# Two-layer graph network on one core: the second layer's scores, softmax and aggregation joined into one pass over batches of 11 blocks

## The chip, the core and the metric

The kernel runs on 1 core of one Trainium2 chip. The metric is the device time of one execution in microseconds. Engines are named as the profile names them: PE is the matrix engine, DVE the vector engine, ACT the scalar engine, POOL the general engine (here above all the issuer of gathers), SP the engine that issues the other transfers.

## The reference, cut to what matters

There are 3,125 nodes with 256 features and 50,000 edges sorted by destination. The first layer (gated messages, summed at the destination) isn't touched. The second layer is attention over the edges:

```python
Q, K, V = ((enh @ W + b).reshape(N, 4, 64) for W, b in ((Wq, bq), (Wk, bk), (Wv, bv)))
mod_k = K[src] + 0.2 * rel_w[edge_relations][:, None, :]
scores = jnp.einsum('ehd,ehd->eh', Q[dst], mod_k) / 64 ** 0.5
seg_max = jax.ops.segment_max(scores, dst, num_segments=N)
ex = jnp.exp(scores - seg_max[dst])
w = ex / jax.ops.segment_sum(ex, dst, num_segments=N)[dst]
agg = jax.ops.segment_sum(w[:, :, None] * V[src], dst, num_segments=N)
msgs = jnp.where(deg[:, None, None] > 0, agg, V)
out = msgs.reshape(N, 256) @ Wo + bo          # then + node_features, layer norm
```

## The kernel before

Edges come in chunks of 256, nodes in windows of 128. A block is one chunk seen against one window; there are 220 blocks, and all edge work runs block by block. Every engine has its own program, written out by hand: `pipeline(engine, stages, count, body)` runs steps u = 0, 1, 2, ..., and in step u each stage of the list, in the order of the list, works on block u minus its lag. So the order of the list is the order in which an engine meets its waits, and a wait at one stage holds all stages behind it, those of the next step too. `after(engine, signal, n)` waits until n signals have come.

The second layer has these parts:

- Projection (L1160 to L1171): K, V and Q of each window. `[K V]` rows go to a table in DRAM (L343), Q stays in SBUF in a high and a low part.
- Scores (220 blocks). SP loads one row of destinations and edge types (L353) and writes the gathered values back to DRAM as `block_values` (L358). POOL gathers 256 rows of `[K V]`, two gathers of 128 rows a block (L430), into 4 slots. PE spreads the row over the partitions (L1183 on), DVE compares it with the partition number to get one-hots (L903), PE adds keys and relations and picks the queries, ACT copies the keys out of PSUM (L643), DVE multiplies (L911) and sums each head's 64 products (L917).
- Softmax over all edges at once (L932 to L964): scores are turned into rows, running maxima go forth and back over each row, carries between rows are added, then one exponential.
- Aggregation (220 blocks). SP brings the values back (L372), DVE weights them (L974), ACT makes the one-hots of the destinations in two steps (`distances1`, L662, and `one_hot1`, L668) and copies the weights beside the values (L656), PE sums with the one-hot, DVE adds the sum to the window's row of `agg` (L982 reads the window's number into a register, L986 adds). The buffers are rings of 5 blocks.
- Output: POOL adds a bias to all of `xs` (L512), scales `agg` (L516), then windows go through the last projection and the norm.

On PE nearly all matmuls are recorded at one helper's line, L1042, transposes at L1045; an f32 product shows as two MATMUL records, an f32r product as one.

Of the kernel before, what the change touches and what calls it, by code (L numbers as in the profile page):

```python
# [13 lines left out]
P = 128  # L14
HEAD = HID // HEADS
CHUNK = 256
# [12 lines left out]
RING = 5  # L29
SHARES = 64  # L30
AGGW = HID + HEADS
assert CHUNKS % 2 == 0 and BLOCKS % SLOTS == 0 and BLOCKS % (2 * RING) == 0


def build(nc, x, src, dst, etype, ea, w1, wg, b_cat, w2, b2, ln0, query_col, wqkv, b_qkv, rel, wo, b_o, ln1, out):
# [6 lines left out]
    kv_tab = nc.dram_tensor("kv_tab", (WPAD * P, 2 * HID), f32, kind="Internal").ap()  # L42
    block_values = nc.dram_tensor("block_values", (BLOCKS // 2, P, 2, 2 * HID), f32, kind="Internal").ap()
    row_tab = nc.dram_tensor("row_tab", (BLOCKS, 2 * CHUNK), bf16, kind="Internal").ap()

    ctx = ExitStack()
    with ctx:
# [13 lines left out]
        ident_r = sb(ctx, "ident_r", [P, P], f32r)  # L61
# [11 lines left out]
        dst_row = sb(ctx, "dst_row", [HALF_B, 2, CHUNK], f32)  # L73
        chunk_i = sb(ctx, "chunk_i", [1, BLOCKS], i32)
        win_i = sb(ctx, "win_i", [1, BLOCKS], i32)
        ends_row = sb(ctx, "ends_row", [HEADS, 2, BLOCKS], f32)
        idx = sb(ctx, "idx", [P, 2, SLOTS, 2], i32)
# [5 lines left out]
        gath = sb(ctx, "gath", [P, SLOTS, 2, 2 * HID], f32)  # L83
# [3 lines left out]
        with l0:  # L87
            w_node = sb(l0, "w_node", [P, 2, 2 * HID], f32)
# [38 lines left out]
            row_b = sb(l0, "row_b", [HALF_B, 2, 2, CHUNK], bf16)  # L127
# [3 lines left out]
        with l1:  # L131
            agg = sb(l1, "agg", [P, WINDOWS, AGGW], f32)
            exp_col = sb(l1, "exp_col", [P, BLOCKS, 2, HEADS], f32)
            rel_parts = sb(l1, "rel_parts", [P, HID], f32r)
            spread = sb(l1, "spread", [P, P], bf16)
            block_row = sb(l1, "block_row", [P, SLOTS, 2, CHUNK], bf16)
            rel_sb = sb(l1, "rel_sb", [P, HEAD], f32)
            wo_hi = sb(l1, "wo_hi", [P, 2, HID], f32r)
            wo_lo = sb(l1, "wo_lo", [P, 2, HID], f32r)
            qt = ExitStack()  # L140
            with qt:
                q_hi = sb(qt, "q_hi", [P, WPAD, HID], f32r)
                q_lo = sb(qt, "q_lo", [P, WPAD, HID], f32r)
                a0 = ExitStack()
                with a0:
                    wqkv_hi = sb(a0, "wqkv_hi", [P, 2, 3 * HID], f32r)
                    wqkv_lo = sb(a0, "wqkv_lo", [P, 2, 3 * HID], f32r)
                    b_qkv_sb = sb(a0, "b_qkv_sb", [P, 3 * HID], f32)
                    qkv_row = sb(a0, "qkv_row", [P, 2, 3 * HID], f32)
                a1 = ExitStack()  # L150
                with a1:
                    hot_t = sb(a1, "hot_t", [P, 2, 2, CHUNK], f32r)
                    key_sb = sb(a1, "key_sb", [P, 2, 2, HID], f32)
                    prod = sb(a1, "prod", [P, 2, 2 * HID], f32)
            a2 = ExitStack()
            with a2:
                s_row = sb(a2, "s_row", [HALF_B, 2, HEADS, CHUNK], f32)
                m_row = sb(a2, "m_row", [HALF_B, 2, HEADS, CHUNK], f32)
                edge_max = sb(a2, "edge_max", [HEADS, 2, BLOCKS], f32)
                run_max = sb(a2, "run_max", [HEADS, 2, BLOCKS], f32)  # L160
                carry = sb(a2, "carry", [HEADS, 2, BLOCKS], f32)
                carry_col = sb(a2, "carry_col", [HALF_B, 2, 2, HEADS], f32)
            a3 = ExitStack()
            with a3:
                values = sb(a3, "values", [P, RING, 2, 2 * HID], f32)
                weighted = sb(a3, "weighted", [P, RING, 2, AGGW], f32)
                dist1 = sb(a3, "dist1", [P, RING, 2, P], f32)
                hot1 = sb(a3, "hot1", [P, RING, 2, P], f32)
                v_in = sb(a3, "v_in", [P, 2, HID], f32)
# [5 lines left out]
                ln1_sb = sb(a3, "ln1_sb", [P, 2, HID], f32)  # L175

# [3 lines left out]
        wo_sb = arriving[:, 6 * HID:8 * HID].rearrange("p (c n) -> p c n", c=2)  # L180


        used = [0]
# [1127 lines left out]
```

## Time and profile before

| | us |
|---|---|
| median of 3 runs | 2142.18 |
| lowest and highest | 2140.08 and 2154.2 |
| the profiled execution, its own time | 2156.49 |
| its span in the profile | 2154.6 |
| PE busy | 1732.6 (80%) |
| DVE busy | 1645.5 (76%) |
| ACT busy | 1135.0 (53%) |
| POOL busy | 1043.5 (48%) |

Busy shares are averages over parts with different limits, so they are to be read part by part. Row times are microseconds from the span's start. Two instructions that stand back to back overlap a little, so what one costs its engine is the distance between two starts, and what a waiting engine sees is the whole duration.

### The profile page before, as it was taken

The page shows a single profiled execution, that of the slowest core. Times are in us where ns is not written, and L with a number is a line of the kernel's source. Part 1 is how long each engine was busy: PE and PEld are TensorE (multiplying, and loading weights), DVE is VectorE, ACT ScalarE, POOL GpSimd, SP SyncE. Part 2 cuts the span into 40 slices and gives each one's busy share as a digit, 9 for nine tenths or more (in the row PEclk, how much of TensorE's full clock was granted, in tenths as well). Part 3 has the DMA queues.
Part 4 walks back from the last instruction along what each step waited for, and adds up shares of the span by engine and source line. Part 5 has one row for each costly group of instructions (what it writes and reads, how often), then busy time and mean ns, then how long its engine had stood idle before and what let it go on. Part 6 is the DMA issues. An engine that isn't in the chain of part 4 may idle for free. (4 is left out here: it accounts for less than half of the span.)

```text
span 2154.6 us, 46785 instructions
## 1 busy us (share of the span) xinstructions
PE 1732.6 (80%) x10754; PEld 1502.2 (70%) x10810; DVE 1645.5 (76%) x3024; ACT 1135.0 (53%) x2898; POOL 1043.5 (48%) x1123
## 2 busy tenths in 40 slices
PE   6799999999999999935877667766777761999984
PEld 3699999999999999934655556555556551655554
DVE  5489889888899888897656666666666567888988
ACT  1377778777888777744411111111111111999953
POOL 0155555555566555559265556666656543000023
PEclk9999999999999999977998988898898995999998
DMA  4456656665666566611487888888888861766643
GB/s 120 169 165 179 179 169 176 174 178 162 178 181 180 163 176 176 175 42 49 145 256 235 242 239 247 249 248 249 245 240 249 250 205 56 234 224 225 230 132 99
DMA packets 203908, 403.45 MB, mean 187 GB/s; under 512 B 29103, under 2 KB 126312, under 8 KB 203880
## 3 DMA queue, kind: packets, MB, share of 16 engines
q0 software_dynamic: 70400, 230.74, 38.0%
q1 hardware_dynamic: 133480, 172.38, 23.9%
q8 instruction: 12, 0.20, 0.0%
q14 instruction: 16, 0.13, 0.0%
HBM read 328.28 MB, written 74.73 MB: 187 GB/s over the span
## 5 line engine op out<-in xcount | busy, mean ns | idle before, releaser
L430 POOL DMA_INDIRECT gath<-edge_in_tab,idx x440 | 464.8, 1056 | 349.1 <-DVE gate_in L816 188.4
L430 POOL DMA_INDIRECT gath<-kv_tab,idx x440 | 417.2, 948 | 275.5 <-issue 108.4
L1042 PE MATMUL bank<-gath,ident 128*128 128x256 f32 x880 | 313.9, 451 | 208.8 <-issue 111.6
L643 ACT COPY key_sb<-bank 128x512 f32<-128x512 f32 x220 | 125.3, 587 | 587.8 <-PE bank L1042 326.9
L1042 PEld LDWEIGHTS bank<-gath,ident 128*128 128x128 f32 x880 | 161.9, 220 | 256.0 <-issue 138.9
L911 DVE TENSOR_TENSOR prod<-bank,key_sb 128x512 f32<-128x512 f32 x220 | 151.3, 688 | 239.7 <-ACT key_sb L643 168.2
L1042 PE MATMUL bank<-weighted,hot 128*128 128x260 f32 x880 | 238.7, 403 | 36.2 <-DVE weighted L974 34.5
L1042 PE MATMUL bank<-w_lo,relu_hi 128*128 128x256 f32 x880 | 250.2, 284 | 0.0
L1042 PE MATMUL bank<-w_hi,relu_lo 128*128 128x256 f32 x880 | 249.8, 284 | 0.0
L1042 PE MATMUL bank<-w_hi,relu_hi 128*128 128x256 f32 x880 | 249.4, 283 | 0.0
L1042 PEld LDWEIGHTS bank<-weighted,hot 128*128 128x128 f32 x880 | 152.6, 191 | 122.3 <-ACT hot L668 57.6
L1042 PE MATMUL bank<-rel_parts,hot_t 128*128 128x256 f32 x440 | 234.1, 532 | 0.0
L569 ACT ACTIVATE relu_hi<-bank 128x512 fp32r<-128x512 f32 x220 | 131.4, 597 | 170.4 <-PE bank L1042 155.2
L1045 PE MATMUL bank<-ident,gath 128*128 128x128 f32 x880 | 170.1, 275 | 23.4 <-DVE ea_parts L803 12.9
L830 DVE TENSOR_TENSOR msg_lo<-msg,msg_hi 128x512 fp32r<-128x512 f32 x220 | 152.9, 695 | 43.1 <-ACT msg_hi L581 21.3
L917 DVE TENSOR_REDUCE exp_col<-prod 128x512 f32 (+1 forms) x220 | 151.0, 686 | 31.2 <-issue 4.9
L974 DVE TENSOR_TENSOR weighted<-values,exp_col 128x512 f32<-128x512 f32 x220 | 163.0, 742 | 12.1 <-DMA values<-block_values 8.5
L1042 PEld LDWEIGHTS bank<-w_hi,relu_lo 128*128 128x128 f32 x880 | 169.8, 193 | 0.0
L825 DVE TENSOR_TENSOR msg<-bank,gate 128x512 f32<-128x512 f32 x220 | 151.2, 688 | 22.6 <-PE bank L1042 6.6
L1042 PEld LDWEIGHTS bank<-w_lo,relu_hi 128*128 128x128 f32 x880 | 168.4, 191 | 0.0
L1042 PEld LDWEIGHTS bank<-w_hi,relu_hi 128*128 128x128 f32 x880 | 168.4, 191 | 0.0
L903 DVE TENSOR_SCALAR hot_t<-bank,iota_part 128x512 fp32r<-128x512 f32 x220 | 163.2, 742 | 2.0 <-remote 2.0
(230 smaller groups left out, 4730.0 us busy)
## 6 DMA issues: line engine op xcount, KB each, us to landing
block_values<-gath SPq DMA_DIRECT2D x220, 256.0 KB
values<-block_values SPq DMA_DIRECT2D x110, 512.0 KB, 3.4
ea_in<-in_ea SPq DMA_DIRECT2D x440, 64.0 KB
gath<-edge_in_tab,idx POOLq DMA_INDIRECT x440
gath<-kv_tab,idx POOLq DMA_INDIRECT x440
edge_in_tab<-node_row SPq DMA_DIRECT2D x26, 256.0 KB, 2.0
kv_tab<-qkv_row SPq DMA_DIRECT2D x26, 256.0 KB, 2.0
block_row<-row_tab SPq DMA_DIRECT2D x220, 1.0 KB
```

The source lines that it names most:

```text
L430: g.indirect_dma_start(gath[:, q, i, :], None, table, bass.IndirectOffsetOnAxis(ap=idx[:, half, q, i:i + 1], axis=0)).then_inc(arrived[q], 16)
L569: s.activation(relu_hi[:, q % 2, :], bank[q % 2][:], ACT.Relu).then_inc(relu_hi_done, 1)
L643: s.copy(key_sb[:, q % 2, :, :].rearrange("p i f -> p (i f)"), bank[2 + q % 2][:]).then_inc(key_copied, 1)
L825: v.tensor_tensor(msg[:, q % 2, :], bank[4 + q % 2][:], gate[:, q % 2, :], ALU.mult).then_inc(msg_done, 1)
L830: v.tensor_tensor(msg_lo[:, q % 2, :, :].rearrange("p i f -> p (i f)"), msg[:, q % 2, :], msg_hi[:, q % 2, :, :].rearrange("p i f -> p (i ...
L903: v.tensor_scalar(hot_t[:, q % 2, :, :].rearrange("p k e -> p (k e)"), bank[q % 2][:], iota_part[:], None, ALU.is_equal).then_inc(hot_t_do ...
L911: v.tensor_tensor(prod[:, q % 2, :], bank[4 + q % 2][:], key_sb[:, q % 2, :, :].rearrange("p i f -> p (i f)"), ALU.mult).then_inc(prod_don ...
L917: v.tensor_reduce(out=exp_col[:, ds(b, 1), :, :].rearrange("p o i h -> p (o i h)"), in_=prod[:, q % 2, :].rearrange("p (j d) -> p j d", d= ...
L974: last = v.tensor_tensor(weighted[:, q % RING, :, 0:HID].rearrange("p i (h d) -> p i h d", h=HEADS), values[:, q // 2, q % 2, :].rearrange ...
L1042: return nc.tensor.matmul(out_, lhsT=lhs, rhs=rhs, start=start, stop=stop)
L1045: return nc.tensor.matmul(out_, lhsT=in_, rhs=ident[:], is_transpose=True, start=start, stop=stop)
```

## The change

Scores, softmax and aggregation become one pipeline over the 220 blocks. Gathered rows of `[K V]` (516 numbers instead of 512: each head's values are followed by a one, which sums the weights) stay in 22 slots in SBUF, until the block's values are weighted; 12 of the slots lie in `xs` and `hs`, which are stored in DRAM before and loaded again at the end. After each 11 blocks the scores, now 44 rows (block, head) of 256 edges, get local maxima, carries, and a running maximum that is passed on to the next batch; `agg` of the window that goes on is rescaled. Keys and queries are now held with features on the partitions: keys are transposed, and heads are summed by a product with `adder`. The row of destinations comes to all partitions by transfer. The core of the diff:

```diff
+BATCH = 11
+KEEP = 2 * BATCH
+BROWS = 2
@@ sync @@
+            sp.wait_ge(x1_done, WPAD)
+            sp.dma_start(rows_tab[0, :, :], xs[:].rearrange("p w f -> p (w f)")).then_inc(rows_saved[0], 16)
             pipeline(sp, [(store_keys_values, 0)], WPAD, 2)
+            sp.wait_ge(h2_done, WPAD)
+            sp.dma_start(rows_tab[1, :, :], hs[:].rearrange("p w f -> p (w f)")).then_inc(rows_saved[1], 16)
...
+                after(sp, hot_t_done, b - BROWS + 1)
+                for half in range(2):
+                    sp.dma_start(block_row[half * RELS:(half + 1) * RELS, slot, :, :].rearrange("p k e -> p (k e)"),
+                                 row_tab[ds(b, 1), half, :].to_broadcast([RELS, 2 * CHUNK])).then_inc(brow_in[slot], 16)
...
-            pipeline(sp, [(load_block_row, 0), (save_values, 3)], BLOCKS, SLOTS)
-            pipeline(sp, [(load_values, 0)], BLOCKS // 2, RING)
+            pipeline(sp, [(load_block_row, 0), (load_steps, 4)], BLOCKS, KEEP)
+            sp.wait_ge(query_fetched, BLOCKS)
+            sp.dma_start(hs_back[:].rearrange("p w f -> p (w f)"), rows_tab[1, :, 0:WINDOWS * HID]).then_inc(rows_back, 16)
+            sp.dma_start(xs_back[:].rearrange("p w f -> p (w f)"), rows_tab[0, :, 0:WINDOWS * HID]).then_inc(rows_back, 16)
+            sp.wait_ge(weighted_done, BLOCKS)
@@ gpsimd @@
+                after(pool, weighted_done, b - KEEP + 1)
+                after(pool, key_ready, b - BATCH + 1)
...
+            pool.wait_ge(rows_back, 2 * 16)
+            pool.wait_ge(ow_in, 4 * 16)
+            g.tensor_tensor(xs_back[:], xs_back[:], ln1_sb[:, 1:2, :].to_broadcast([P, WINDOWS, HID]), ALU.add).then_inc(beta1_added, 1)
@@ scalar @@
+            def fetch_query(k, q):
+                b = KEEP * k + q
+                w = act.value_load(win_i[0:1, ds(b, 1)], min_val=0, max_val=WINDOWS - 1)
+                after(act, query_ready, b - 1)
+                s.copy(q_now[:, q % 2, :, :].rearrange("p t f -> p (t f)"),
+                       q_tab[:, ds(w, 1), :, :].rearrange("p o t f -> p (o t f)")).then_inc(query_fetched, 1)
...
+            def distances1(k, q):
+                b = KEEP * k + q
+                after(act, agg_ready, b - 1)
+                for i in range(2):
+                    last = s.activation(hot1[:, q % 2, i, :], iota_node[:], ACT.Square, bias=rel_col[:, ds(b, 1), i], scale=-1.0)
+                last.then_inc(dist1_done, 1)
...
+            pipeline(act, [(fetch_query, 0), (copy_keys, 1), (copy_scores, 3), (copy_weights, 7), (distances1, 17), (one_hot1, 18),
+                           (exponents, 6)], BLOCKS, KEEP)
@@ vector @@
+                v.tensor_scalar(hot_t(q).rearrange("p k e -> p (k e)"), block_row[:, slot, :, :].rearrange("p k e -> p (k e)"),
+                                iota_part[:], None, ALU.is_equal).then_inc(hot_t_done, 1)
...
+                v.tensor_tensor_scan(m_row[0:ROWS, 0, :], steps_in[0:ROWS, half, 0:CHUNK], s_row[0:ROWS, :], -BIG, ALU.add, ALU.max)
...
+            pipeline(dve, [(one_hot_t, 0), (products, 1), (weight_values, 18), (rescale, 20), (add_agg, 20), (local_maxima, 3),
+                           (running_maxima, 4), (segment_maxima, 5)], BLOCKS, KEEP)
@@ tensor @@
+                for c in range(2):
+                    to = bank[q % 2][:, c * CHUNK:(c + 1) * CHUNK]
+                    for i in range(2):
+                        tr(to[:, i * P:(i + 1) * P], kept(q, c * P, P)[:, i, :], i == 0, False)
+                    last = mm(to, rel_parts[:, c * P:(c + 1) * P], hot_t(q)[:, 1, :], False, True)
+                last.then_inc(key_ready, 1)
+                pe.wait_ge(query_fetched, b + 1)
+                after(pe, prod_done, b - 1)
+                for c in range(2):
+                    to = bank[2 + q % 2][:, c * CHUNK:(c + 1) * CHUNK]
+                    for t in range(2):
+                        last = mm(to, q_now[:, q % 2, t, c * P:(c + 1) * P], hot_t(q)[:, 0, :], t == 0, t == 1)
+                last.then_inc(query_ready, 1)
...
+            def add_heads(k, q):
+                    last = mm(bank[4][:, 0:CHUNK], adder[:, at:at + P], kept(q, 0, CHUNK)[:, c, :],
...
+            def aggregate(k, q):
+                pe.wait_ge(hot1_done, b + 1)
+                pe.wait_ge(weighted_done, b + 1)
+                after(pe, agg_added, b - 1)
...
+            pipeline(pe, [(keys_and_queries, 0), (ends_of_rows, 4), (carry_to_rows, 5), (add_heads, 2), (aggregate, 19), (weights_to_columns, 6)],
+                     BLOCKS, KEEP)
```

`local_maxima`, `running_maxima` and `segment_maxima` (DVE) run once in 11 blocks: 2 scans of 256 numbers and 2 small instructions; 2 scans of 11 and 8 small ones; 2 scans of 256, a copy and a subtraction of 256. `ends_of_rows`, `carry_to_rows` and `weights_to_columns` (PE) are 1 and 3 tiny f32 products and 2 transposes a batch; ACT has `copy_scores`, `exponents` (2 instructions) and `copy_weights` a batch. Ahead of the edge work of the first layer there are 3 more passes of DVE over the rows of destinations and types, one of ACT, two of POOL, and 8 small stores by SP that stand before the stores of the first layer's node table.

## Rows read from the trace of the kernel before

**Rows 1.** Busy time by stretch: start and end, length, engines with instructions, PEclk, DMA share, GB/s
```profile
56.00:919.00 863.00, 829.83 (x6667) 806.83 (x6665) 740.01 (x1339) 659.63 (x1557) 475.38 (x495) 0.99 0.60 174
1062.00:1772.00 710.00, 501.02 (x2364) 412.04 (x2418) 439.08 (x658) 125.91 (x221) 426.92 (x494) 0.88 0.81 244
...
1831.00:2084.00 253.00, 238.64 (x880) 152.50 (x880) 225.04 (x438) 237.18 (x857) 0.00 (x0) 0.99 0.66 219
```

**Rows 2.** Timeline, POOL in the score stage
```profile
1731.13 0.95 POOL L430 DMA_INDIRECT gath<-kv_tab,idx  x1 [0.30 <-issue]
```

**Rows 3.** Timeline of PE, score stage: start, duration, what, [idle before <-releaser]
```profile
1700.77 1.22 PE L1042 MATMUL bank<-gath,ident 128*128 128x256 f32 x2 [3.92 <-issue]
...
1707.62 0.47 PE L1042 MATMUL bank<-rel_parts,hot_t 128*128 128x256 f32 x1
...
1708.17 0.47 PE L1042 MATMUL bank<-rel_parts,hot_t 128*128 128x256 f32 x1
...
1708.48 0.28 PE L1042 MATMUL bank<-q_hi,hot_t 128*128 x1
...
1708.60 0.28 PE L1042 MATMUL bank<-q_lo,hot_t 128*128 x1
...
1709.99 0.70 PE L1042 MATMUL bank<-gath,ident 128*128 128x256 f32 x2 [0.65 <-issue]
```

**Rows 4.** Timeline of ACT in the aggregation stage
```profile
1842.05 0.51 ACT L668 ACTIVATE hot<-dist,one_col 128x256 f32<-128x256 f32 x1
1842.46 0.68 ACT L662 ACTIVATE dist<-iota_node,rel_col 128x128 f32<-128x128 f32 x2
1843.04 0.19 ACT L656 COPY weighted<-exp_col 128x8 f32<-128x8 f32 x1
```

**Rows 5.** Timeline of PE in the aggregation stage
```profile
1908.96 1.11 PE L1042 MATMUL bank<-weighted,hot 128*128 128x260 f32 x4 [0.23 <-DVE weighted L974]
```

**Rows 6.** Group of ACT, first layer: count, busy, mean ns, idle before
```profile
L581 ACT CAST msg_hi<-msg 128x512 fp32r<-128x512 f32 x98 | 59.9, 611 | 0.0
```

**Rows 7.** Timeline, first layer: PE after a stall, and two transposes
```profile
915.50 0.38 PE L1042 MATMUL bank<-b_parts,share 128*128 128x256 f32 x1 [0.53 <-DVE relu_lo L808]
...
917.27 0.38 PE L1045 MATMUL bank<-ident,gath 128*128 128x128 f32 x2
```

**Rows 8.** The reading of the window's number, DVE's queue: ns min/median/max
```profile
L982 DVEq TENSOR_LOAD <-win_i x220: 298/302/329, 1818.6 to 2083.2; - x110
```

**Rows 9.** Groups of DVE, the page's part 5
```profile
L911 DVE TENSOR_TENSOR prod<-bank,key_sb 128x512 f32<-128x512 f32 x220 | 151.3, 688 | 239.7 <-ACT key_sb L643 168.2
L903 DVE TENSOR_SCALAR hot_t<-bank,iota_part 128x512 fp32r<-128x512 f32 x220 | 163.2, 742 | 2.0 <-remote 2.0
```

**Rows 10.** Timeline of DVE, start of the kernel
```profile
10.03 0.33 DVE L730 TENSOR_SCALAR chosen<-iota_b,first_b 98x220 f32<-98x220 f32 x1
```

**Rows 11.** Timeline of DVE, the softmax stage
```profile
1777.74 4.62 DVE L937 TENSOR_TENSOR_SCAN m_row<-agg,s_row 110x1024 f32<-110x1024 f32 x2
...
1791.00 0.38 DVE L950 TENSOR_TENSOR carry<-run_max,agg 4x219 f32<-4x219 f32 x1
...
1793.41 0.17 DVE L953 COPY carry_col<-bank 110x16 f32<-110x16 f32 x1 [1.74 <-PE bank L1042]
```

**Rows 12.** DMA issues: KB each, us to landing
```profile
xs<-in_x SPq DMA_DIRECT2D x1, 3328.0 KB, 13.3
...
w_node<-in_w SPq DMA_DIRECT2D x1, 256.0 KB, 13.2
```

**Rows 13.** Timeline, start of the aggregation stage
```profile
1816.08 14.19 POOL L512 TENSOR_TENSOR xs<-xs,ln_sb 128x6656 f32<-128x6656 f32 x1 [8.00 <-DMA ln_sb<-in_ln]
1817.38 15.24 DVE L974 TENSOR_TENSOR weighted<-values,exp_col 128x512 f32<-128x512 f32 x4 [8.50 <-DMA values<-block_values]
```

**Rows 14.** Timeline, end of the aggregation stage
```profile
2084.02 0.42 DVE L986 TENSOR_TENSOR agg<-agg,bank 128x260 f32 x1 [0.40 <-DVE agg L986]
...
2085.93 16.40 POOL L516 TENSOR_TENSOR agg<-agg,inv 128x256 f32<-128x256 f32 x25 [255.66 <-DVE inv L995]
```

More of the change, by code:

```diff
@@ L156, in build @@
[L156 to L162, printed above, removed]
+                    kept_more = sb(a1, "kept_more", [P, KEEP - 12, 2 * KVW], f32)
@@ L163, in build @@
+                    weight_col = sb(a1, "weight_col", [P, 2, 2, ROWS], f32)
+                    weighted = sb(a1, "weighted", [P, 2, 2, VALW], f32)
+                    hot1 = sb(a1, "hot1", [P, 2, 2, P], f32)
             a3 = ExitStack()
             with a3:
[L165 to L168, printed above, removed]
@@ L443, in _ @@
+            with pool.Fori(0, (BLOCKS - SLOTS) // (2 * SLOTS)) as k:
+                for u in range(2 * SLOTS):
+                    gather_node_rows(2 * SLOTS * k + SLOTS, u, 1 - u // SLOTS, 2 * k + 1 + u // SLOTS)
             pool.wait_ge(lw_in, 3 * 16)
@@ L472, in _ @@
             pool.wait_ge(wqkv_lo_done, 1)
[L474 to L490 removed]
+            whole = into[:, 1, :]
             step(g.memset(follows[:], 0.0))
@@ new lines, in add_agg @@
+            def add_agg(k, q):
+                b = KEEP * k + q
+                w = dve.value_load(win_i[0:1, ds(b, 1)], min_val=0, max_val=WINDOWS - 1)
+                dve.wait_ge(agg_ready, b + 1)
+                if q % BATCH == 0:
+                    dve.wait_ge(rescaled, 2 * k + q // BATCH + 1)
+                else:
+                    dve.wait_ge(agg_added, b)
+                rows = agg[:, ds(w, 1), :].rearrange("p o f -> p (o f)")
+                v.tensor_tensor(rows, rows, bank[6 + q % 2][:, 0:VALW], ALU.add).then_inc(agg_added, 1)
@@ L927, in _ @@
+            dve.wait_ge(consts, 3)
             dve.wait_ge(segments_known, 1)
[L928 to L937 removed]
@@ L938, in _ @@
-            for r in range(2):
-                rows = m_row[:, r, :, :].rearrange("p h e -> p (h e)")
-                last = v.tensor_tensor_scan(rows[:, ::-1], reset[:, r, HEADS * CHUNK:0:-1], rows[:, ::-1], -BIG, ALU.add, ALU.max)
-            last.then_inc(local_done, 1)
-            dve.wait_ge(lends_ready, 1)
-            for i in range(2):
-                last = v.tensor_copy(edge_max[:, i, :], bank[4 + i][0:HEADS, 0:BLOCKS])
-            step(last)
-            v.tensor_tensor_scan(run_max[:, 0, :], through[:, 0, :], edge_max[:, 1, :], -BIG, ALU.add, ALU.max)
@@ new lines, in keys_and_queries @@
+                last.then_inc(query_ready, 1)
+            def add_heads(k, q):
+                b = KEEP * k + q
+                g, turn = 2 * k + q // BATCH, q % BATCH
+                pe.wait_ge(prod_done, b + 1)
+                if turn == 0:
+                    after(pe, scores_copied, g)
+                for c in range(2):
+                    at = FIRST_COL - HEADS * turn - 2 * c
+                    last = mm(bank[4][:, 0:CHUNK], adder[:, at:at + P], kept(q, 0, CHUNK)[:, c, :],
+                              turn == 0 and c == 0, turn == BATCH - 1 and c == 1)
+                if turn == BATCH - 1:
+                    last.then_inc(scores_ready, 1)
```

603 lines of the change are left out of this document (321 added, 282 removed).

## The prediction

> **What bounds the kernel now.** I read the busy time by stretch first [rows 1]. The second layer's edge work runs from 1062 to 2084.4 us, where the last sum is added to `agg` [rows 14]: 1022 us, nearly half of the span. It has three parts: scores, 710 us for 220 blocks or 3.23 us a block; softmax over all edges, 59 us to 1831, in which no engine is full; aggregation, 253 us or 1.15 a block. In the scores no engine is full either (PE 501 of 710 us, DVE 439, POOL 427), but the DMA engines are at 0.81: the values are gathered, written back and later read again. Aggregation is full on PE, ACT and DVE together. On the face of it much is to be won: the transfers of values and the softmax's 59 us go.
>
> The sum is made against the profiled execution, 2156.5 us (span 2154.6 and 1.9 around it). That is 14 us above the median of the runs; I add the difference that I find to the median.
>
> **The change part by part: what each engine has to do for a block.**
> - POOL: a gather takes 0.95 and 0.30 us lies ahead of it [rows 2], so 2.5 us a block, as before.
> - PE: an f32 product of 256 columns and an f32r one take 0.55 together (1707.62 to 1708.17), an f32r one 0.12 (1708.48 to 1708.60) [rows 3], so an f32 one 0.44. Two transposes take 0.38 as a pair, some 0.22 between starts [rows 7]. Keys: 4 transposes and 2 f32r products, 0.7. Queries: 4 f32r, 0.48. `add_heads`: 2 f32, 0.88. `aggregate`: the same 1.11 as before from first start to last end [rows 5]. In all 3.0 to 3.2.
> - DVE: products and weighting 0.6 each (0.69 lasting, overlapping by 0.09) [rows 9], `add_agg` 0.34 (0.42 lasting [rows 14]), the one-hot 0.5 (below): 2.0. Once a batch 6 us more: scans cost 2.25 ns a number (4.62 us for 2 of 1024) [rows 11], so 4 of 256 are 2.6 us with their fixed part; some 12 small ones at 0.17 to 0.2, the latter with a self-wait; a subtraction and a rescaling at 0.4. 0.55 a block.
> - ACT: `distances1` 0.58 (1842.46 to 1843.04), `one_hot1` 0.41 to the next start [rows 4], two copies of 512 at 0.5 to 0.61 [rows 6]: 2.1.
>
> So by work alone a step would be 3.2 us, PE's, and 220 of them some 700 us against 1022. That is what I do not forecast, because of the order of the waits.
>
> **The loop between PE and ACT.** `hot1` now has 2 buffers, not 5. In step u ACT's `distances1` works on block u-17 and waits until block u-19 is aggregated. PE does block u-19 in the same step u, behind everything else. Behind `distances1` ACT has `one_hot1` and then step u+1, which begins with `fetch_query(u+1)`; and PE's queries of step u+1 wait for that. So per step, one after the other, with PE at full clock:
> - end of `aggregate` to ACT: 0.08, an estimate, since no row gives a handover by itself (bounds 0.05 and 0.15);
> - `distances1` 0.58, `one_hot1` 0.41 [rows 4];
> - `fetch_query`: 512 numbers SBUF to SBUF, 0.61 [rows 6]. Ahead of it ACT's queue reads the window's number, a load of 0.30 [rows 8] and register work behind it; most of it lies beside the 0.99 above; I take 0.1 exposed (bounds 0 and 0.4);
> - handover 0.08, the first product after a stall lasts 0.38 and not 0.28 [rows 7], so 0.1;
> - queries 0.48, `add_heads` 0.88, `aggregate` 1.11.
>
> Sum 4.43 us. Only the keys (0.8) lie outside of it, beside ACT's part. DVE has the step's products 0.5 after the fetch, ends its round at 2.6, and would be late only from 3.6 on.
>
> Once a batch more comes. DVE's three pieces (1.6, 1.8, 1.95 us, in three following steps, ahead of the next one-hot) exceed the 1.0 of slack: later keys by 0.55, 0 and 0.25. PE's small products add 0.2 and 0.6. `weights_to_columns` waits for ACT's two exponentials, which stand behind `one_hot1`: 0.9 with the keys behind it. Rescaling 0.1. Together 2.6 us, 0.24 a block. The turn of the loop once in 22 blocks and small bubbles add 0.08: in aggregation the turn left PE idle 0.23 us more than its neighbours once in 10 blocks [rows 5]. **4.75 us a step.** Bounds: 4.3 (no exposure, batches hidden but for PE's own products) and 5.2 (0.4 exposed, all pieces in full).
>
> The one-hot of DVE was 0.74 with its input in PSUM [rows 9]; now the input is in SBUF. A compare of 220 numbers against a column from SBUF took 0.33 [rows 10], less than a two-tensor instruction of 219 numbers, 0.38 [rows 11]. Bounds for 512: 0.33 and 0.74; I take 0.5. The Trainium skill ("VectorE: DVE Perf Modes", Mode 2×_2P) says that a one-source instruction with input and output in SBUF goes at two numbers a cycle; the pair of rows agrees. By it the one-hot would be 0.5; were the rule not to hold here, 0.74, and the two batch pieces that reach the chain would come 0.25 later each, 20 x 0.5 = 10 us.
>
> **The sum of the edge part.**
> - Start. `hs` (3.3 MB) is stored on SP's queue behind the last K, V store at 1058, and the first rows of destinations stand behind it. A 3.3 MB load took 13.3 us, and 256 KB issued right behind it also 13.2 [rows 12], so a queue keeps its order. Here gathers share the engines. Bounds 8 and 30 us after 1062; I take 22.
> - Fill: until step 20 nothing is aggregated; PE 2.2 and POOL 2.5 a step with a head start: 20 x 2.3 = 46.
> - Steady: 200 x 4.75 = 950.
> - Drain, 18 steps: `one_hot1` stands behind the waiting `distances1`, so aggregate 1.11, 0.58, 0.51 and two handovers: 2.35 x 18 = 42, and 2 for the last sum.
>
> Together 1062 against 1022: +40.
>
> **Around it.** The bias on `xs` (L512) takes 14.2 us [rows 13]. It used to run at the start of aggregation, where it stopped DVE (4 weightings took 15.2 us); now it waits for loads that SP issues only when the last block is weighted. Loads to start was 7 to 8 us then [rows 13]; I take 6, then 14.2 x 25/26 = 13.7, so POOL scales `agg` 19.7 after the last weighting, or 17.5 after the last sum, where it was 1.5 [rows 14]: +16 (bounds 12 and 22). The loads of `hs_back` and `xs_back`, 2 x 13 us [rows 12], lie beside the drain's 42. Ahead of the first layer: 3 passes of DVE, one of ACT, two of POOL and 8 issues before the first table store: +4 (0 to 8). Storing `xs` lies beside the statistics and the first projection; the softmax's preparation on POOL shrinks, but was beside the projection anyway: 0. All told +60: 2142 + 60 = **2202 us**.
>
> **The rivals.**
> 1. *The loop is shorter than the sum* (4.3 to 4.45 us a step; handovers and batches hidden). For it: my batch prices are estimates. Against: 3.9 of the 4.43 are durations of rows. At 4.3 it is 90 us less than 950: 2112; break-even lies at 4.45.
> 2. *The loop doesn't close*, the step is PE's work (3.2 to 3.5): 200 x 3.4 = 680, 270 less; 1930. For it: all busy sums, and 0.81 of DMA share going away. Against: the lags 17 and 19, and the count that `distances1` waits for.
> 3. *The clock*: PE was busy 0.71 in the scores with its clock at 0.88, 0.96 in the first layer at 0.99 and 0.94 in aggregation at 0.99 [rows 1]. After an idle of 3.9 us two records took 1.22 us, after 0.65 us 0.70 [rows 3]. The new idle stretches are some 1 us, 1.6 at a batch, so I take full clock. At 0.88 PE's 2.57 us in the loop grow by 0.35: 200 x 0.35 = 70 us more, 2272.
> 4. *A transfer becomes the bound*: destination rows have only 2 slots. From one one-hot to the row for the next but one: issue, landing, waits. It decides above 9.5 us, two steps; landings of some 4 to 8 us [rows 13] don't reach that. At 11 us for two steps it would be 5.5 a step: 2350.
>
> **How the numbers follow.** The forecast with 4.55 to 5.0: 0.48. Rival 1: 0.24, half of it within 1%. Rival 2: 0.13. Rival 3 and the upper part of the bounds: 0.12. Rival 4: 0.03. Below 1% this kernel's measurement can hardly tell from none. Faster by over 1% is rival 2 and the lower part of rival 1 and a step of 4.35 or less: 0.24. Within 1% (4.35 to 4.55): 0.16. Slower: 0.60. The range takes 4.3 to 5.2 a step with the start's and the tail's bounds: 2105 to 2290.
>
> **What would show it.** ACT's `distances1` idle in most steps until PE's `aggregate`; PE idle about 0.9 us between keys and queries, released by the copy into `q_now`; starts of the copy 4.4 us apart between batches and up to 5.5 at them; DMA share under 0.6; POOL idle half the time; PEclk 0.95 or more; the bias on `xs` 6 us after the last weighting, and nothing on DVE after it until POOL is through. I am wrong if copies into `q_now` come less than 4.2 us apart, if PE is busy over 0.85 of the steady stretch, or if DVE's one-hot waits for rows of destinations.

## The result, and the profile after

The changed kernel took 2211.64 us (median of 4 runs, 2203.85 to 2216.14), the kernel before, run beside it, 2147.3 us (4 runs, 2140.08 to 2154.2). The ratio is 1.030, with a 95% interval of 1.024 to 1.035: slower, 9.6 us above the forecast of 2202 us and inside its range. The profiled execution took 2203.85 us, with a span of 2202.1.

The page of the changed kernel, parts 1, 2 and 4:

```profile
PE 1747.2 (79%) x11627; PEld 1541.9 (70%) x11627; DVE 1511.4 (69%) x3174; ACT 1244.4 (57%) x2977; POOL 1041.8 (47%) x1077
...
PE   6799999999999999628477777777777777777644
...
PEclk9999999999999999859699999999999999999858
DMA  4456656666665666223745555555455454555313
...
PE 58%; issue 15%; DVE 10%; ACT 8%; DVEq 3%; ACTq 2%; DMA 2%; another core or an unknown queue 1%; POOL 1%; SPq 0%; POOLq 0%
```

The second half of the PE row is a row of sevens at a full clock, with DMA at half: nothing is full for 1000 us. The busy time by stretch (columns as in [rows 1]) and the waits of the steady part say the same with numbers:

```profile
1200.00:2000.00 800.00, 590.09 (x3241) 473.84 (x3240) 434.30 (x988) 368.84 (x919) 345.17 (x359) 0.98 0.51 142
```

```profile
ACT hot L713 <- PE bank L1131: 358.6, 149, 5.6
POOL kept_more L466 <- DVE weighted L1039: 188.6, 76, 5.1
...
PE bank L1131 <- ACT q_now L678: 64.7, 80, 1.1
PEld bank L1134 <- DVE ht_hi L967: 57.6, 58, 1.9
```

(The row of waits: who waited, for whom, us in total, times, longest. `kept_more`, `xs` and `hs` are the places of the kept rows; `ht_hi` and `ht_lo` hold DVE's one-hots, by turns.) Where [rows 1] had a DMA share of 0.81 and a clock of 0.88 in the scores, there is now 0.51 and 0.98. ACT, busy 46% of the time, waits 359 of 800 us for PE, always at `distances1` (L713). PE in turn waits for ACT's copy into `q_now` (L678). Two engines that wait for each other in every step, neither of them full: such a picture suggests a loop, which experiments 1 and 2 test. One round of it, from the timeline:

```profile
1536.99 0.69 ACT L713 ACTIVATE hot<-iota_node,rel_col 128x128 f32<-128x128 f32 x2 [2.20 <-PE bank L1131]
...
1537.59 0.49 ACT L719 ACTIVATE hot<-hot,one_col 128x256 f32<-128x256 f32 x1
...
1537.99 0.60 ACT L678 CAST q_now<-q_tab 128x512 fp32r x1
...
1538.65 0.75 PE L1131 MATMUL bank<-ht_lo,q_now 128*128 128x256 f32 x4 [0.19 <-ACT q_now L678]
...
1539.23 1.03 PE L1131 MATMUL bank<-hs,adder 128*128 128x256 f32 x4
...
1540.10 1.04 PE L1131 MATMUL bank<-weighted,hot 128*128 128x260 f32 x4
...
1541.27 0.69 ACT L713 ACTIVATE hot<-iota_node,rel_col 128x128 f32<-128x128 f32 x2 [2.19 <-PE bank L1131]
```

The chain to follow is distances, one-hot, query, queries, heads, aggregate, distances: 1541.27 less 1536.99 is 4.28 us. The distances from one start of the copy into `q_now` to the next, in us, for two batches of 11 steps of this kernel (read off the timeline, blocks 110 to 131):

```
7.29 4.27 4.62 4.82 5.02 4.87 4.70 4.27 4.29 4.29 4.28   sum 52.7
4.28 4.28 4.62 4.63 6.63 4.65 4.68 4.27 4.27 4.26 4.52   sum 51.1
```

Five steps of a batch are late, 2.6 us in an ordinary batch (49.7 less 11 x 4.28); and seven times, 22 blocks apart, there is a step some 3 us longer, like the 7.29. The 199 steps from block 20 (1133.5 us) to block 219 (2056.8) took 4.64 us each.

The 6.63 in the second row is a step of another kind. PE stood idle for 1.29 and 1.35 us ahead of the keys of two neighbouring steps, behind DVE's pieces, and then ran at its lower clock for about one step:

```profile
1613.25 0.44 PE L1134 MATMUL bank<-ident,xs 128*128 128x128 f32 x2 [1.35 <-issue]
...
1615.05 1.75 PE L1131 MATMUL bank<-xs,adder 128*128 128x256 f32 x4
1616.59 1.94 PE L1131 MATMUL bank<-weighted,hot 128*128 128x260 f32 x4
```

The same products last 1.03 and 1.04 us in the round above. The granted clock of the stretch 1613.5 to 1618 us is 0.71. Four steps of the stage are like this one; in most batches the same idle stretches leave the clock at its upper level. Six of the seven long steps 22 blocks apart hold products at the lower clock as well; in the one of 7.29 us DVE's one-hot comes late and then PE's products take longer:

```profile
1543.60 0.49 DVE L967 TENSOR_SCALAR ht_hi<-block_row,iota_part 128x512 fp32r<-128x512 bf16 x1 [2.85 <-issue]
...
1546.40 1.38 PE L1131 MATMUL bank<-hs,adder 128*128 128x256 f32 x4
```

In the seventh (from 1338.8 us) the one-hot is late by 2.79 us and PE keeps its upper level: that step takes 5.85 us, 1.6 over the ordinary one, where the six with the lower clock take 3.0 to 3.4 over it.

Two places more, the drain and the tail:

```profile
2071.36 1.12 PE L1131 MATMUL bank<-weighted,hot 128*128 128x260 f32 x4
2073.66 2.10 PE L1131 MATMUL bank<-weighted,hot 128*128 128x260 f32 x4 [1.18 <-ACT hot L719]
```

```profile
2117.62 0.42 DVE L1063 TENSOR_TENSOR agg<-agg,bank 128x260 f32 x1 [1.10 <-PE bank L1131]
...
2120.72 13.10 DVE L1082 TENSOR_TENSOR b_o_parts<-b_o_sb,b_o_parts 64x256 fp32r<-64x256 f32 x1 [1.22 <-ACT wo_hi L729]
```

```profile
2119.89 13.65 POOL L542 TENSOR_TENSOR xs_back<-xs_back,ln_sb 128x6400 f32<-128x6400 f32 x1 [75.13 <-DMA wo_sb<-in_wo]
2133.50 16.82 POOL L546 TENSOR_TENSOR agg<-agg,inv 128x256 f32<-128x256 f32 x25
```

From 2073.66 on the same four products of `aggregate` last 2.10 us, not 1.12, and a step takes 3.28 us: the granted clock of the stretch 2084 to 2117 us is 0.50, the lower of its two levels. Behind the last sum POOL spends 13.65 us on the addition of beta, and a subtraction of 64x256 on DVE beside it takes 13.10.

### The profile page after: what moved, and what is told of

Its sections match the earlier page's. It is cut to its first block, busy times and chain, and to the rows that moved or that the text cites. A ratio compares the mean times of both kernels' runs of the same rounds, so it can differ in the third digit from the quotient of the medians.

```text
span 2202.1 us, 46103 instructions
## 1 busy us (share of the span) xinstructions
PE 1747.2 (79%) x11627; PEld 1541.9 (70%) x11627; DVE 1511.4 (69%) x3174; ACT 1244.4 (57%) x2977; POOL 1041.8 (47%) x1077
## 4 chain that ended last, share of the span: by engine, by line
PE 58%; issue 15%; DVE 10%; ACT 8%; DVEq 3%; ACTq 2%; DMA 2%; another core or an unknown queue 1%; POOL 1%; SPq 0%; POOLq 0%
PE bank L1131 51%; PE bank L1134 7%; ACT q_now L678 3%; ACT hot L713 2%; ACTq L676 1%; DVEq L1056 1%; POOL xs L501 1%; DVE relu_lo L866 1%; ACT hot L719 1%; DVE ht_hi L967 1%; DVE b_o_parts L1082 1%; DVE stats L803 1%; DVEq L893 1%; ACT kept_more L684 1%
## 5 line engine op out<-in xcount | busy, mean ns | idle before, releaser
L713 ACT ACTIVATE hot<-iota_node,rel_col 128x128 f32<-128x128 f32 x440 | 152.6, 394 | 530.5 <-PE bank L1131 453.7
L466 POOL DMA_INDIRECT kept_more<-kv_tab,idx x200 | 198.2, 991 | 269.6 <-DVE weighted L1039 226.5
L974 DVE TENSOR_TENSOR kept_more<-bank,kept_more 128x512 f32<-128x512 f32 x100 | 69.1, 691 | 217.7 <-issue 104.7
L1131 PEld LDWEIGHTS bank<-weighted,hot 128*128 128x128 f32 x880 | 177.0, 203 | 52.7 <-ACT hot L719 25.5
L466 POOL DMA_INDIRECT hs<-kv_tab,idx x120 | 124.7, 1039 | 144.0 <-DVE weighted L1039 117.5
L466 POOL DMA_INDIRECT xs<-kv_tab,idx x120 | 114.9, 958 | 143.6 <-DVE weighted L1039 116.1
L1131 PE MATMUL bank<-ea_parts,w_edge_hi 128*128 128x256 f32 x440 | 161.6, 367 | 0.0
L609 ACT ACTIVATE gate<-gate_in 128x512 f32<-128x512 f32 x220 | 139.3, 633 | 24.9 <-DVE gate_in L874 24.5
L1134 PE MATMUL bank<-ident,kept_more 128*128 128x128 f32 x400 | 81.0, 295 | 90.9 <-DVE ht_hi L967 47.0
L866 DVE SCALAR_TENSOR_TENSOR relu_lo<-bank,relu_hi 128x512 fp32r<-128x512 f32 x220 | 149.6, 680 | 3.9 <-ACT relu_hi L603 3.9
```

Of the source, the lines that this page charges most:

```text
L466: g.indirect_dma_start(kept(u, 0, KVW)[:, i, :], None, kv_tab, bass.IndirectOffsetOnAxis(ap=idx1[:, half, u % BATCH, i:i + 1], axis=0)).th ...
L609: s.activation(gate[:, q % 2, :], gate_in[:, q % 2, :], ACT.Sigmoid).then_inc(gate_done, 1)
L713: last = s.activation(hot1[:, q % 2, i, :], iota_node[:], ACT.Square, bias=rel_col[:, ds(b, 1), i], scale=-1.0)
L866: v.scalar_tensor_tensor(relu_lo[:, q % 2, :], in0=bank[q % 2][:], scalar=0.0, in1=relu_hi[:, q % 2, :], op0=ALU.max, op1=ALU.subtract).th ...
L974: v.tensor_tensor(kept(q, 0, CHUNK), bank[2 + q % 2][:].rearrange("p (c e) -> p c e", c=2), kept(q, 0, CHUNK), ALU.mult).then_inc(prod_don ...
L1131: return nc.tensor.matmul(out_, lhsT=lhs, rhs=rhs, start=start, stop=stop)
```

## The experiments

These ran on three chips, one for each group, that agree within 0.5% and are faster than that of the pair above: the kernel before took 2048 us there (first group of four) and 2039 us (second and third group), and the changed kernel 2155. So each is compared by its ratio to the kernel before, and within a group by times. The changed kernel itself ran in the second group only; a difference against its 2155 us from another group is good to some 10 us, and the value by ratios stands beside it. All starts are those of the copy into `q_now`.

### 1. The lags of the one-hot

```diff
-(distances1, 17), (one_hot1, 18),
+(distances1, 18), (one_hot1, 19),
```

> Starts from the changed kernel; ACT does distances1 for block u-18 and one_hot1 for block u-19 in step u, one step later than before each, nothing else. distances1 then waits for the aggregate that PE did in step u-1, not in the same step. Loop theory: the chain aggregate, distances, one-hot, copy of the query, queries is cut; the step falls from 4.28 us between batches to PE's own work, 3.2 to 3.5 us, some of the batch extra of 2.6 us stays; 200 steps at 3.6 instead of 4.65 give 210 us less than the changed kernel: about 2000 us (1950 to 2060). Rival, the step is set by batches, handovers or transfers: starts stay at 4.2 or more, 2180 us or more. Rival, the loop is cut but destination rows with 2 slots or the gathers take over at 3.8 to 4.2 a step: 2090 to 2130 us.

Measured: 1907.5 us, ratio 0.931 (0.928 to 0.935). Starts are 2.89 us apart between batches. The gain is 248 us against the 2155 of the changed kernel (258 by ratios); I had expected 210. In the timeline `distances1` still waits, but no longer for the end of PE's same step:

```profile
1296.18 0.70 ACT L713 ACTIVATE hot<-iota_node,rel_col 128x128 f32<-128x128 f32 x2 [0.68 <-PE bank L1131]
1296.79 0.50 ACT L719 ACTIVATE hot<-hot,one_col 128x256 f32<-128x256 f32 x1
1297.19 0.60 ACT L678 CAST q_now<-q_tab 128x512 fp32r x1
```

```profile
1086.00:1764.00 678.00, 618.77 (x3777) 541.15 (x3776) 523.99 (x1143) 432.94 (x1073) 426.81 (x408) 0.99 0.70 198
```

PE is busy 0.91 of the stretch, against 0.74 in the changed kernel. The loop was the cause of the slow step, and the version with this one edit beats the kernel before by 7%.

### 2. Twice the distances, and 3. twice the key transposes

Both add work: the first on ACT inside the loop, into columns that nothing reads, the second on PE outside of it.

```diff
+                for i in range(2):
+                    s.activation(spare[:, i * P:(i + 1) * P], iota_node[:], ACT.Square, bias=rel_col[:, ds(b, 1), i], scale=-1.0)
                 for i in range(2):
                     last = s.activation(hot1[:, q % 2, i, :], iota_node[:], ACT.Square, bias=rel_col[:, ds(b, 1), i], scale=-1.0)
```

> Starts from the changed kernel; distances1 first makes the same two distances once more into unused columns, 0.58 us more on ACT in each of 220 steps, behind the wait for aggregate. Loop theory: all of it lies in the loop, steps between batches 4.86 instead of 4.28, in all 219 x 0.58 = 127 us more, about 2335 us (2310 to 2350), although ACT was busy only 46% of the stretch. Rival, the step is set by something outside of ACT: less than 40 us more.

Measured: 2314.2 us, 1.131 (1.129 to 1.134). Starts between batches 4.86: 0.58 more, the whole of the added work, on an engine that was busy less than half of the time. The total grew by 159 (152 by ratios), not 127. The other 25 to 30 us are steps that are 1.5 to 2 us longer, mostly those behind DVE's batch pieces, and there PE ran at its lower clock:

```profile
1752.59 1.04 PE L1134 MATMUL bank<-weighted,hot 128*128 128x260 f32 x4
...
1756.01 0.73 PE L1134 MATMUL bank<-ht_lo,q_now 128*128 128x256 f32 x4 [1.41 <-ACT q_now L678]
1756.85 1.92 PE L1134 MATMUL bank<-xs,adder 128*128 128x256 f32 x4
1758.56 1.94 PE L1134 MATMUL bank<-weighted,hot 128*128 128x260 f32 x4
```

PE is idle for 1.41 us ahead of the queries in an ordinary step, where the changed kernel has 0.83, and the clock was granted 0.89 in such a stretch (1503 to 1566 us). This is the mechanism of rival 3 of the prediction. The changed kernel shows it too, in ten steps of 199; here it is far more frequent.

```diff
                     for i in range(2):
+                        tr(to[:, i * P:(i + 1) * P], kept(q, c * P, P)[:, i, :], True, True)
+                    for i in range(2):
                         tr(to[:, i * P:(i + 1) * P], kept(q, c * P, P)[:, i, :], i == 0, False)
```

> Starts from the changed kernel; PE makes the four key transposes of each block twice, about 0.5 us more of PE's work in each step, ahead of the queries. Loop theory: PE was idle 0.83 us between keys and queries, so the starts between batches stay at 4.28; only in the 4 or 5 steps of a batch in which the keys are late is it paid, up to 20 x 2 = 40 us: 2212 to 2252 us. Rival, PE's work sets the step: 220 x 0.5 = 110 us more, 2320 us.

Measured: 2186.16 us, 1.069 (1.067 to 1.071), 31 us more than the changed kernel (24 by ratios). Starts between batches stay at 4.28; the late steps of a batch are longer (50.1 to 51.4 us for a batch without a turn of DVE's loop, 49.5 to 49.7 in the changed kernel). Two additions of about the same length, one on the emptier and one on the busier engine, cost 159 and 31 us. What decides is the place in the loop, not how busy the engine is.

### 4. The tail

```diff
+            for i in range(2):
+                sp.dma_start(ln1_sb[:, i, :], ln1[i:i + 1, :].to_broadcast([P, HID])).then_inc(rows_back, 16)
             sp.wait_ge(weighted_done, BLOCKS)
...
-            g.tensor_tensor(xs_back[:], xs_back[:], ln1_sb[:, 1:2, :].to_broadcast([P, WINDOWS, HID]), ALU.add).then_inc(beta1_added, 1)
+            for w in range(WINDOWS):
+                last = g.tensor_tensor(xs_back[:, w, :], xs_back[:, w, :], ln1_sb[:, 1, :], ALU.add)
+            last.then_inc(beta1_added, 1)
```

In memory `ln1_sb` moved to the place behind `xs_back`, where it covers only `q_tab`.

> Starts from the changed kernel; gamma and beta are loaded right behind xs_back, as soon as the last query is fetched, and POOL adds beta in 25 pieces of one window during the drain. Theory: POOL scales agg 1 to 2 us after the last sum instead of 17 (the whole addition took 13.65 us there, and DVE's small subtraction beside it 13.1), drain unchanged or up to 3 us longer: 14 us less than the changed kernel (10 to 17), about 2198 us. Rival, the pieces hold DVE up in the drain as the whole addition did, or the loads land too late: gain under 5 us.

Measured: 2143.16 us, 1.047 (1.045 to 1.049). That is 12 us less than the changed kernel by times and 21 by ratios (the groups differ by 0.4% in the kernel before); from last sum to end its trace has 71.6 us where experiment 3, with the tail untouched, has 84.8: 13 us.

```profile
2033.65 20.03 POOL L542 TENSOR_TENSOR xs_back<-xs_back,ln_sb 128x256 f32<-128x256 f32 x25 [32.39 <-DMA ln_sb<-in_ln]
2077.74 16.89 POOL L547 TENSOR_TENSOR agg<-agg,inv 128x256 f32<-128x256 f32 x25 [24.05 <-DVE inv L1081]
```

```profile
2077.69 0.42 DVE L1083 TENSOR_TENSOR b_o_parts<-b_o_sb,b_o_parts 64x256 fp32r<-64x256 f32 x1
```

The pieces take 20 us beside the drain, the drain's steps stay at 3.28 us, and DVE's subtraction takes 0.42 instead of 13.10. The Trainium skill ("SBUF — State Buffer", "SBUF: two separate sides") says that VectorE and GpSimd share a port pair, and that a GpSimd instruction which reads SBUF and a VectorE instruction with two SBUF inputs exclude each other for their whole length. The rows agree: DVE's subtraction, with two inputs in SBUF, was held beside one addition of 13.65 us; beside the 25 pieces DVE's weightings, of the same kind, lasted up to 1.29 us instead of 0.70, and the wait for PE hid that.

### 5 and 6. Both kernels on the other chip

> The changed kernel itself, beside the others: on the chip of the first four experiments the kernel before took 2048, 100 us less than in the pair of the prediction. With the tail experiment at 2143 and its trace showing a tail 13 us shorter, I expect 2157 us (2145 to 2170). Then the doubled key transposes cost 20 to 30 and the doubled distances 150. If instead the chip does not matter for the ratio (1.03), it would be 2110 us on a chip where the kernel before takes 2048.

> The kernel before itself, for a trace of it on this chip. Theory: what differs between chips is the speed of gathers and transfers, so the difference sits in the score stage (710 us, DMA share 0.81) and in the first layer, and aggregation (1.15 us a block, bound by PE, ACT and DVE) stays at 253 us. Rival: TensorE's clock differs, and it sits where PE is busy and was granted 0.88.

The changed kernel took 2155.42 us, 1.057 (1.055 to 1.060), and the kernel before, as a run of its own, 2037.8 us. The same two programs are 3.0% apart on one chip and 5.7% on the other. The trace of the kernel before there, three stretches (first layer, scores, aggregation):

```profile
56.00:900.00 844.00, 815.47 (x6760) 807.32 (x6758) 770.24 (x1359) 670.00 (x1578) 485.97 (x496) 0.98 0.60 178
1013.00:1654.00 641.00, 454.36 (x2364) 375.53 (x2418) 440.89 (x657) 129.38 (x221) 426.73 (x494) 0.96 0.88 270
1713.00:1966.00 253.00, 238.10 (x880) 152.14 (x880) 225.67 (x440) 237.11 (x857) 0.00 (x0) 0.99 0.64 219
```

Against [rows 1] the scores take 641 us instead of 710 at 270 GB/s instead of 244, and aggregation takes the same 253. The first layer ends 50 us earlier too (weights of the next phase are loaded at 900.5 us, not at 950.2). So the kernel before gains 118 us where transfers count; the changed one, held by its loop, has the same 4.28 between batches and 4.67 on the mean of the same 16 batches on both chips (821 us for 176 steps) and gains only in the first layer (weights of the next phase at 903.6 us, not at 935.5) and in the start and fill of the edge part, 20 us. The clock (0.96 instead of 0.88 in the scores) differs as well, but PE is idle for a quarter of that stretch; which of the two came first isn't told apart.

### 7 and 8. Both edits, and the one-hot of DVE a step ahead

Lags and tail together:

> Both edits together: distances and one-hot one step later, and gamma and beta loaded early with beta added in pieces in the drain. They touch different stretches, so the gains add: 13 us less than with the lags alone, 1894 us on the chip where that took 1907. Rival, the drain or the loads after it become late instead: no gain beside the lags alone.

Measured: 1890.41 us, 0.926 (0.924 to 0.929); the gains add. Then every stage but `one_hot_t` one step later, on all engines:

```diff
-(one_hot_t, 0), (products, 1), (weight_values, 18), (rescale, 20), (add_agg, 20), (local_maxima, 3),
+(one_hot_t, 0), (products, 2), (weight_values, 19), (rescale, 21), (add_agg, 21), (local_maxima, 4),
```

> As the two edits together, and every stage but DVE's one-hot one step later, so that the one-hot is ready a step ahead of the keys. With the lags alone three steps of each batch take 4.2, 4.65 and 3.9 us instead of 2.89, keys waiting for a one-hot that stands behind DVE's pieces of the maxima. Theory: lateness of the one-hot by itself is the price; DVE has 2.0 us of work a step and 6 us a batch, 28 of 32 us, so it catches up: of 4.1 us a batch 2 to 3 go, 20 x 2.5 = 50 us less than the two edits, and one more step of 3 us: 1850 us on the same chip. Rival, products and the weighting behind the pieces are late as well (they stay where they are): less than 20 us.

Measured: 1823.99 us, 0.894 (0.892 to 0.896), 66 us less than the version beside it; I had expected 40 to 50. A batch takes 33.0 to 35.0 us instead of 35.3 to 42.6. PE is busy for 560 of 567 us:

```profile
1083.00:1650.00 567.00, 560.09 (x3509) 506.21 (x3508) 468.49 (x1065) 404.05 (x996) 396.08 (x390) 1.00 0.75 219
```

### 9. The query a step ahead: a miss

From the changed kernel, every stage but `fetch_query` one step later; `distances1` waits for PE's same step as before.

```diff
-(fetch_query, 0), (copy_keys, 1), (copy_scores, 3), (copy_weights, 7), (distances1, 17), (one_hot1, 18),
+(fetch_query, 0), (copy_keys, 2), (copy_scores, 4), (copy_weights, 8), (distances1, 18), (one_hot1, 19),
```

> Starts from the changed kernel; the wait of distances1 for the aggregate of PE's same step stays as it is, but the query of a block is copied one step ahead: every stage of every engine except fetch_query runs one step later. Loop theory: the link from one-hot through the copy of the query to PE's queries is cut; what is left of the loop is aggregate, distances, one-hot, 2.3 us, less than PE's 2.89 of work, so it is as fast as with the lags alone, 0.93 of the kernel before (0.92 to 0.94). Rival, the buffer of the one-hot and its wait is what costs, the query has no part in it: ratio stays above 1.04.

Measured: 2121.49 us, 1.040 (1.038 to 1.042): 34 us less than the changed kernel, where I had expected 250. Neither theory fits: the loop theory is far off, and the rival gave the query no part at all, though its bound of 1.04 is just where the ratio came out. The starts come 2.89 and 4.57 us apart in turn outside of the batch steps, which is 3.73 on the mean:

```profile
1469.74 0.44 PE L1134 MATMUL bank<-ident,hs 128*128 128x128 f32 x2 [1.45 <-DVE ht_lo L967]
...
1473.00 0.69 ACT L713 ACTIVATE hot<-iota_node,rel_col 128x128 f32<-128x128 f32 x2 [2.48 <-PE bank L1131]
...
1474.00 0.60 ACT L678 CAST q_now<-q_tab 128x512 fp32r x1
1474.51 0.57 ACT L684 COPY hs<-bank 128x512 f32<-128x512 f32 x1
...
1475.11 0.69 DVE L974 TENSOR_TENSOR hs<-bank,hs 128x512 f32<-128x512 f32 x1 [2.54 <-ACT hs L684]
```

PE no longer waits for the query. It waits for DVE's one-hot, DVE's round waits for ACT's copy of the keys, and that copy stands in ACT's queue behind the same waiting `distances1`. The chain now goes over three engines and two steps. I worked it out only after the run: distances 0.6, one-hot 0.4, query 0.5, keys 0.6 on ACT; products 0.6, weighting 0.6, sum 0.35 and one-hot 0.5 on DVE; and PE's whole step of 2.9: 7.05, with four handovers of 0.1 some 7.4, against 7.46 for two steps in the trace. That the sum comes out is no proof, since it was made for the trace; no run cuts this chain at the copy of the keys. In the batch steps DVE's pieces of 1.6 to 1.95 us lie in this chain too, and they come out at 4.6 to 5.1 as before. Once in 22 steps one takes 9.4 us, against 7.3 to 7.7 in the changed kernel; why it grew was not looked into. The prediction's list of who waits for ACT's round was right but too short.

### 10. DVE's loop written out straight

> Starts from the changed kernel; DVE's loop over 22 blocks is written out straight, no turn. In the changed kernel one step in 22 is 3.1 us longer, with DVE idle 2.9 us ahead of the one-hot with nothing that releases it, 7 to 9 times. Theory: it is the turn of DVE's own loop; 9 x 3 = 27 us less, ratio 1.044 where the changed kernel has 1.057. Rival, it is the turn of another queue (SP's, which brings the rows): no change, 1.057. Third, straight code costs as much in many places: above 1.057.

Measured: 2126.05 us, 1.043 (1.041 to 1.045), 29 us less. In the changed kernel (experiment 5) DVE's waits in the steady part have this line:

```profile
DVE ht_hi L967 <- issue: 20.3, 7, 3.1
```

In the straight version no such line is left, and a batch takes 49.5 to 49.8 us, but for one of 51.2. So the long step is the turn of DVE's own loop over 22 blocks. The loop proper starts at block 44, since the first 44 blocks are written out ahead of it, so it turns 7 times. In the trace of experiment 5 the seven steps with a turn are 22 us longer than ordinary ones. Each of them holds products at PE's lower clock, behind an idle of 3.05 to 3.3 us; by the one turn of the first section's trace that had none (5.85 us), about half of the 22 us is the clock's. Three single steps at the lower clock, 1.7 us longer each, are there besides, and one is left in the straight version. Together that is 26 of the 29 us. The Trainium skill ("Runtime: NRT & Kernel Launch", "Instruction fetch mechanics") says that a taken branch to a target outside of the pages at hand stalls the engine until they are fetched. DVE's idle of 2.9 us a turn agrees with such a stall, though no row here shows the fetch itself.

### 11 and 12. PE kept busy in the drain, and all edits together

```diff
+            def keep_warm(k, q):
+                b = KEEP * k + q
+                if isinstance(b, int) and BLOCKS - 17 <= b < BLOCKS - 1:
+                    pe.wait_ge(key_copied, BLOCKS)
+                    for i in range(4):
+                        mm(bank[0][:, i * P:(i + 1) * P], ident[:], head_of[:], True, True)
```

> Starts from the version with one-hot, lags and tail edits (0.894); in the drain PE does four useless products of 128 columns in f32, 0.22 each at full clock, into an unused bank behind each aggregate, where it was idle 1.2 us a step and its clock was granted half. Theory: the drain's 3.28 us a step are the loop aggregate, distances, one-hot with aggregate at half clock (2.1 instead of 1.04); kept busy PE keeps its clock, 2.3 a step, 16 x 1 = 16 us less, ratio 0.886. Rival, the clock falls all the same: the products last 1.8 a step and stand ahead of the next aggregate, 0 to 10 us more.

Measured: 1811.45 us, 0.888 (0.887 to 0.890), 12.5 us less than experiment 8 (12 by ratios). First the drain of experiment 8, then the one with the useless products:

```profile
1720.79 2.10 PE L1132 MATMUL bank<-weighted,hot 128*128 128x260 f32 x4 [1.18 <-ACT hot L720]
1724.07 2.10 PE L1132 MATMUL bank<-weighted,hot 128*128 128x260 f32 x4 [1.18 <-ACT hot L720]
```

```profile
1732.62 1.05 PE L1132 MATMUL bank<-head_of,ident 128*128 128x128 f32 x8
1733.97 1.15 PE L1132 MATMUL bank<-weighted,hot 128*128 128x260 f32 x4 [0.29 <-ACT hot L720]
1734.95 1.05 PE L1132 MATMUL bank<-head_of,ident 128*128 128x128 f32 x8
1736.30 1.14 PE L1132 MATMUL bank<-weighted,hot 128*128 128x260 f32 x4 [0.29 <-ACT hot L720]
```

Granted clock 1.00, and 2.33 us a step instead of 3.28: more work on PE, and each step 1 us shorter. Last, the same with DVE's loop straight:

> As the one before, and DVE's loop written out straight. Theory: in the version with all edits but these two the turn costs 0.8 to 1.5 us, 9 times: 9 us less than the one before, ratio 0.882. Rival as for the straight loop of the changed kernel: no change or more.

Measured: 1799.25 us, 0.882 (0.881 to 0.884), 12 us less. PE has no idle time left in the steady stretch:

```profile
1083.00:1650.00 567.00, 567.00 (x3580) 516.02 (x3578) 493.59 (x1081) 410.34 (x1015) 439.85 (x397) 1.00 0.75 223
```

This version is 11.8% faster than the kernel before.

## Why the prediction was right, point by point

- *The loop* (forecast 4.43 us): it exists and ends where it was said to; 4.28 between batches. From the copy of the query to PE's queries it took 0.66 us where 0.79 was forecast (the reading of the window's number wasn't exposed), PE's three products took 2.49 instead of 2.57, and the handover from `aggregate` to ACT 0.13 instead of 0.08. Experiments 1 and 2 show the loop by cutting it and by lengthening it.
- *Batches* (2.6 us): 2.6, though with another split: the delays of the three steps behind DVE's pieces were 0.34, 0.54 and 0.74, and there were two more of 0.6 and 0.4.
- *Turn and bubbles* (0.08 a step): too small. The seven steps with a turn are 21 us longer than ordinary ones, 0.10 a step, and four single steps at PE's lower clock add 7 us, 0.03 a step.
- *The step* 4.75: 4.64. The loop was 0.15 shorter than forecast, and the turn and the clock took some of that back.
- *Start and fill* (22 + 46 = 68): 86.7, from 1046.8 to 1133.5 us. The start was shorter than forecast (the first one-hot comes at 1056.5, 9.7 us in) and the fill longer, 77 us for 46. Block 20 came 3.5 us from the forecast 1130 by luck only, since the part began 15 us earlier than it was taken to. In the fill DVE waits 14 us ahead of the products at 1079.8 and PE 12.5 ahead of 1080.95, for something that the profile doesn't name; the cause stays open. On the chip of experiment 5 the same piece is 21 us shorter: from POOL's first copy of gather indices to ACT's first distances 58.8 us (1014.47 to 1073.31), here 80.3 (1045.42 to 1125.72). *The one-hot of DVE* (0.5): 0.48.
- *Drain* (44 us): 57. The step of it that failed is the term 1.11 for `aggregate`: at half clock it is 2.1. Experiment 11 shows that the idle time was the reason. The prediction had weighed the clock for the steady part, where it was granted 0.98 on the mean, and not for the drain, where PE has nothing but `aggregate` to do.
- *Tail* (+16): 84.1 us from last sum to end against 70.2, +14.
- *Ahead of the edge part* (+4): here −15. In this execution the first layer ended 15 us earlier than in the profiled one of the kernel before. On the faster chips the same point came 4.5 us later than in the kernel before (905.07 us in experiment 1, 900.54 in experiment 6), which is the forecast +4. The first layer's length varies by more than the term is large, on chips and perhaps between executions; why is left open.
- In sum the edge part took 1071 us from 1046.8 to the last sum, against 1022 before: +49 for a forecast of +40. That these two lie so close is luck in part: start and fill were 19 us longer than forecast and the drain 13, and the steps 22 shorter. With tail +14 and ahead −15 it is +48 between the two profiled executions, and +64 between the medians, since the profiled execution of the kernel before was 9 us above its median and that of the changed kernel 8 below its own. So the agreement with the forecast +60 is closer by the medians than the terms are one by one.
- *The rivals*: rival 2, no loop, was right on what would be possible: 3.06 us a step was reached in experiment 8, not in the change as it stands. Rival 3 came true in a small part: ten of the 199 steps hold products at the lower clock, behind two idle stretches of 1.2 to 1.5 us in neighbouring steps or one of 3 us. An estimate from their lengths: four single steps at 1.7 us and six turns at 1.4 to 1.8 over the turn without it, some 16 us, where the rival had 70. The prediction took full clock for idle stretches of 1.6 us at a batch. Rival 4 did not happen; with the loop gone, DVE waited 46 us of 540 for rows of destinations in experiment 8, so it is the next thing in line behind PE.
- Two sums of the prediction are a little off: the durations of rows in the loop add up to 4.1 us, not 3.9, and 5.2 us a step alone gives 2292 us, just above the upper end of the range.

## What to carry to other kernels

Work out per step not only what each engine has to do but who waits for whom within the step; where a buffer with 2 places is freed by the last work of the other engine's same step, everything behind that wait in the queue joins the chain, and the sum round it, not the busiest engine, is the step. Here one step more of lag, at no cost of memory, turned 6% slower into 7% faster, each against the kernel before, on two chips of nearly the same speed. To repair such a chain, move the instruction that waits (experiment 1); moving one of those behind it left the others behind it (experiment 9).

## What the runs showed of the hardware

- TensorE can be given useless work and the step gets shorter: 2.33 us instead of 3.28 in the drain, because the clock stays at its upper level (granted 1.00 instead of 0.50). With idle stretches of 1.18 us ahead of 1.1 us of work it fell to the lower one.
- PE fell to its lower clock within a stage that was granted 0.98 on the mean: after two idle stretches of 1.2 to 1.5 us in neighbouring steps, or one of 3 us, its products took up to 1.9 instead of 1.0 us for about a step. The same stretches did not do it every time: most pairs and one of the seven turns left it at the upper level.
- The turn of a loop of 22 long steps left DVE idle for 2.9 us each time, 7 times, and writing it out straight gave 29 us back, with most of the falls of the clock.
- The score stage of the kernel before ran at 244 GB/s on one chip and 270 on another, 69 us apart, while a kernel held by a loop of waits had the same step on both. A ratio measured on one chip may not hold on the next: 1.030 here, 1.057 there.
